# Half the depth of the first output product moved into the graph attention, with two score tiles loaded ahead

## What is computed

```python
edge_index = jnp.stack([src, dst])
xn = _layernorm(x, axis=-1)
x = x + _L0_gnn_ref(xn, edge_index, ...) + _L0_mix_ref(xn[None], ...)[0]
x = x + _L0_ffn_ref(_layernorm(x, axis=-1)[None], ...)[0]

# _L0_mix_ref: linear attention, heads of 64, ends in
out = out.transpose(0, 2, 1, 3).reshape(Bq, Tq, -1)     # 1250 x 1024
return out @ Wo.T + bo

# _L0_gnn_ref: attention over the edges, 4 heads of 64, ends in
out = jax.ops.segment_sum(alpha[..., None] * xl[src], dst, num_segments=n)
out = out.reshape(n, HID)                               # 1250 x 256
return out @ W_up
```

## Time and profile before

| what | value |
|---|---|
| device time, median of 3 runs (2938.48 to 2946.75) | 2941.86 us |
| span of the profiled execution | 2940.1 us |
| TensorE matmul busy over the span | 2668.4 us (91%) |
| `mix0` | 322 to 743 us |
| `out0` | 743 to 902 us |
| `gat_phase` | 902 to 1164 us |

### The profile page before, as it was taken

One profiled execution on the slowest core, in us unless ns is written; L12 is line 12 of the kernel. 1 busy time (PEld: TensorE's weight loads), 2 busy tenths in 40 slices (PEclk: granted clock), 3 DMA queues, 4 the chain that ended last, 5 costly groups with the idle time before them and its releaser, 6 DMA issues. The chain is left out here.

```text
span 2940.1 us, 51469 instructions
## 1 busy us (share of the span) xinstructions
PE 2668.4 (91%) x19570; PEld 2513.2 (85%) x19570; DVE 1606.8 (55%) x3190; ACT 961.0 (33%) x1941; POOL 791.7 (27%) x772
## 2 busy tenths in 40 slices
PE   6677899999885998699979999999999999999788
PEld 6455799999885997588869999899998999999577
DVE  7677677787634886655553222254545332225655
ACT  4466433333203563244431010243434120001243
POOL 0567766777640332122200000000000001100054
PEclk9888999999996998799989999999999999999989
DMA  8933433433739882477753111121112653224382
GB/s 242 289 100 110 115 114 96 116 100 82 209 104 212 225 202 97 117 184 202 193 123 107 40 36 52 30 61 31 58 34 91 185 159 93 65 63 122 121 280 75
DMA packets 202069, 362.93 MB, mean 123 GB/s; under 512 B 33654, under 2 KB 135246, under 8 KB 200595
## 3 DMA queue, kind: packets, MB, share of 16 engines
q1 hardware_dynamic: 165733, 278.89, 32.5%
q0 software_dynamic: 36112, 80.96, 10.9%
HBM read 272.97 MB, written 98.15 MB: 126 GB/s over the span
## 5 line engine op out<-in xcount | busy, mean ns | idle before, releaser
L180 PE MATMUL mix_bank<-sums_w_hi,layer_act_hi 128*125 128x256 f32 x1280 | 359.9, 281 | 0.0
L181 PE MATMUL mix_bank<-sums_w_lo,layer_act_hi 128*125 128x256 f32 x1280 | 359.2, 281 | 0.0
L182 PE MATMUL mix_bank<-sums_w_hi,layer_act_lo 128*125 128x256 f32 x1280 | 358.7, 280 | 0.0
L3184 POOL TENSOR_TENSOR sage_add<-sage_add,sage_bias 125x256 f32<-125x256 f32 x40 | 29.4, 736 | 1193.1 <-DMA sage_add<-resid 1192.9
L181 PEld LDWEIGHTS mix_bank<-sums_w_lo,layer_act_hi 128*125 128x125 f32 x1280 | 237.8, 186 | 0.2
L182 PEld LDWEIGHTS mix_bank<-sums_w_hi,layer_act_lo 128*125 128x125 f32 x1280 | 237.9, 186 | 0.0
L180 PEld LDWEIGHTS mix_bank<-sums_w_hi,layer_act_hi 128*125 128x125 f32 x1280 | 237.7, 186 | 0.1
L567 POOL DMA_INDIRECT scored_ring<-xl,edge_idx x168 | 176.6, 1051 | 157.5 <-issue 138.2
L574 POOL DMA_INDIRECT scores<-edge_e,edge_idx x168 | 174.6, 1039 | 138.5 <-DMA scores<-edge_e,edge_idx 98.9
L567 POOL DMA_INDIRECT scored_ring<-xr,edge_idx x168 | 172.6, 1027 | 51.6 <-issue 51.0
L924 PE MATMUL count_pa<-count_hot_s,count_hot_d 125*125 125x416 bf16 (+1 forms) x624 | 137.5, 383 | 29.9 <-DVE count_hot_s L834 27.8
(11 more groups left out here) (638 smaller groups left out, 8575.0 us busy)
## 6 DMA issues: line engine op xcount, KB each, us to landing
ffn_raw<-in_L_ffn_w_dram SPq DMA_DIRECT2D x16, 2048.0 KB, 13.0
scores<-targets_hole SPq DMA_DIRECT2D x40, 546.9 KB
ffn_raw<-in_L_ffn_W_dram SPq DMA_DIRECT2D x16, 1024.0 KB
gat_sc<-scores SPq DMA_DIRECT2D x6, 2187.5 KB
lasting_raw<-in_L_mix_w_qkv_dram SPq DMA_DIRECT2D x24, 512.0 KB, 3.9
scored_ring<-scores SPq DMA_DIRECT2D x4, 2187.5 KB
layer_slab<-in_L_gnn_W_neigh_dram SPq DMA_DIRECT2D x7, 1024.0 KB
layer_slab<-in_L_gnn_W_self_dram SPq DMA_DIRECT2D x7, 1024.0 KB
```

The lines of the kernel that those rows point to most:

```text
L180: pe.matmul(out, lhs[0], rhs[0], start=first, stop=False)
L181: pe.matmul(out, lhs[0], rhs[1], start=False, stop=False)
L182: return pe.matmul(out, lhs[1], rhs[0], start=False, stop=last)
L3184: pool.tensor_tensor(add[:, u % 2, :], add[:, u % 2, :], bb[:, g * SLAB:(g + 1) * SLAB], ALU.add) \
```

## The change

The depth of the first output product is cut in two. The near half (`NEAR` = 4 parts of 128) stays in `out0`. The far half (`FAR` = 4) is written by `mix0` and `out0` to a new DRAM tensor `far`, laid out by node tile, and multiplied in `gat_phase` inside `product`. `gat_phase` loads the far half of `Wo` (`wide_raw`), turns it by TensorE in eight rounds (`turn_far`, `far_rounded` on ScalarE, `far_rest` on VectorE) during its tile 0, and per tile loads 256 KB of `far` (`mixed`) and splits it (`mix_rounded` on ScalarE, `mix_rest` on GpSimd). The `idle` matmuls are gone. To make room, `DEEP` goes from 3 to 2. The second score tile now has a buffer open since `out0`, and both tiles are loaded there, behind the wait for the last scatter. Batches of edges: 26 in `count_phase`, 13 per two slabs in `mix0`, 6 in `out0`.

```diff
-COUNT_BATCHES = 24
+COUNT_BATCHES = 26
-DEEP = 3
+DEEP = 2
-SLAB_BATCHES = 6
-MIX_END = COUNT_BATCHES + SLAB_BATCHES * (D // (2 * HD))
+SLAB_BATCHES = 13
+MIX_END = COUNT_BATCHES + SLAB_BATCHES * (D // (4 * HD))
...
     def load(self, sp, edges):
         edges.landed(sp)
-        move_rows(sp, self.ring[0:R, 0:N * HEADS], self.rows, self.s_in)
+        move_rows(sp, self.ring[0:R, 0:N * HEADS], self.rows[0], self.s_in)
+        move_rows(sp, self.second[:, :, :].rearrange("p s h -> p (s h)"), self.rows[1], self.s_next)
...
+        w_far = [ph.sb(f"far_{s}", [P, FAR, D], F32R) for s in ("hi", "lo")]
+        mix_raw = ph.sb("mix", [P, 2, FAR, R], F32)
+        mix = [ph.sb(f"mix_{s}", [P, 2, FAR, R], F32R) for s in ("hi", "lo")]
...
+                def mixed(t):
+                    if t >= 2:
+                        sp.wait_ge(s_mlo, t - 1)
+                    sp.dma_start(mix_raw[:, t % 2, :, :], far[t]).then_inc(s_mix[t % 2], 16)
...
+                sp.dma_start(wide_raw[:, :, :], wo.rearrange("(i p) k -> p i k", p=P)[:, :, NEAR * P:D]).then_inc(s_wide, 16)
...
                 for t in range(T):
                     if t + DEEP < T:
                         tile(t + DEEP)
+                        mixed(t + 2)
...
+                def mix_rest(t):
+                    pool.wait_ge(s_mhi, t + 1)
+                    pool.tensor_tensor(mix[1][:, t % 2, :, :], mix_raw[:, t % 2, :, :], mix[0][:, t % 2, :, :].bitcast(F32),
+                                       ALU.subtract).then_inc(s_mlo, 1)
...
+                def far_rest(*rounds):
+                    for i in rounds:
+                        k, c = ROUNDS[i]
+                        cols = slice(c * BANK, (c + 1) * BANK)
+                        dve.wait_ge(s_fhi, i + 1)
+                        dve.tensor_tensor(w_far[1][:, k, cols], pr[:, :], w_far[0][:, k, cols].bitcast(F32), ALU.subtract) \
+                           .then_inc(s_flo, 1)
...
+                def turn_far(i):
+                    k, c = ROUNDS[i]
+                    if i:
+                        pe.wait_ge(s_flo, i)
+                    else:
+                        pe.wait_ge(s_wide, 16)
+                    for j in range(4):
+                        ins = pe.transpose(pr[:, j * P:(j + 1) * P], wide_raw[:, 4 * c + j, k * P:(k + 1) * P], ident[:, :])
+                    ins.then_inc(s_ftr, 1)
...
+                    for k in range(FAR):
+                        mm3(pe, pr[0:R, :], [x[:, t % 2, k, :] for x in mix], [x[:, k, cols] for x in w_far], k == 0, False)
                     for k in range(KH):
-                        ins = mm3(pe, pr[0:R, :], [x[:, k, :] for x in gat], [x[:, k, c * BANK:(c + 1) * BANK] for x in up],
-                                  k == 0, k == KH - 1)
+                        ins = mm3(pe, pr[0:R, :], [x[:, k, :] for x in gat], [x[:, k, cols] for x in up], False, k == KH - 1)
...
-                    if 1 <= t < T:
-                        idle(16)
...
-                    if 1 <= t < T:
-                        idle(10)
...
+                    if first is not None and g == 2:
+                        sp.wait_ge(s_quot, NC)
+                        sp.dma_start(far_part(far, SLABS - 1), output.last.rearrange("p (t r) -> p t r", r=R)).then_inc(s_far, 16)
+                        first.load(sp, edges)
...
-                        if first is not None and g == NSLAB - 1 and half:
-                            first.load(sp, edges)
...
-                        for k in range(KD):
-                            ins = part_product(g, t, k, k == 0, k == KD - 1)
+                        for k in range(KS):
+                            ins = part_product(g, t, k, k == 0, k == KS - 1)
```

More of the change, by code:

```diff
@@ L1057, in keep, with gat_phase @@
         dve.tensor_reduce(self.prob[:, n, :], every, AX.X, ALU.add).then_inc(self.s_prob, 1)
-def gat_phase(nc, first, scores, at, xl, ident, w_up, bias, part, dst, normed, gate_w, prob_out):
+def gat_phase(nc, first, scores, at, xl, ident, w_up, wo, bias, part, far, dst, normed, gate_w, prob_out):
     with Phase(nc, "gat") as ph:
-        sc = [first.tile] + [ph.sb(f"sc{i}", [R, N, HEADS], F32) for i in range(1, DEEP)]
+        sc = [first.tile, first.second]
         cnt = ph.sb("cnt", [R, DEEP, T, R], F32)
@@ L1121, in _ @@
                 tile(1)
+                mixed(0)
                 move_rows(sp, bb, bias.rearrange("(o n) -> o n", o=1).to_broadcast([R, D]), s_bias)
                 rows(0)
-                for t in range(2, DEEP):
-                    tile(t)
+                mixed(1)
                 for t in range(1, ROWS - 1):
@@ L1928, with __init__ @@
 class OutputSlabs:
-    QUARTERS = 4
-    def __init__(self, ph, wo, flip, ahead):
+    def __init__(self, ph, wo, flip, ahead, room=None):
         self.wo, self.flip, self.ahead = wo, flip, ahead
-        self.parts = [ph.sb(f"part{i}", [P, N], F32) for i in range(ahead)]
+        self.depth, self.chunks = (NEAR, 2) if flip else (KD, 4)
+        lent = [] if room is None else [room[:, 0:N], room[:, N:2 * N]]
+        self.parts = [ph.sb(f"part{i}", [P, N], F32) for i in range(ahead - len(lent))] + lent
         self.s_parts = ph.sems("part", ahead)
@@ L1958, in load_parts, with output_phase @@
             sp.dma_start(self.parts[k][:, :], mixt[k * P:(k + 1) * P, :]).then_inc(self.s_parts[k], 16)
-def output_phase(nc, name, act_hi, act_lo, mixt, output, ident, resid, dst, edges=None, turn=None, load=None, room=None, run=None, stage=0, first=None, near=None):
-    WC = OutputSlabs.QUARTERS
+def output_phase(nc, name, act_hi, act_lo, mixt, output, ident, resid, dst, edges=None, turn=None, load=None, run=None, stage=0, first=None, near=None, far=None):
+    WC, KS = output.chunks, output.depth
     DEEP = 4
@@ L1973, in output_phase @@
     with Phase(nc, name, run) as ph:
-        part = output.parts + ([room[:, 0:N], room[:, N:2 * N]] if room is not None else [])
-        part += [ph.sb(f"part{i}", [P, N], F32) for i in range(len(part), DEEP)]
-        w = [output.w0, [ph.sb(f"w1_{s}", [P, KD, SLAB], F32R) for s in ("hi", "lo")]]
+        part = output.parts + [ph.sb(f"part{i}", [P, N], F32) for i in range(output.ahead, DEEP)]
+        w = [output.w0, [x[:, NEAR:KD, :] for x in output.w0] if flip else
+             [ph.sb(f"w1_{s}", [P, KS, SLAB], F32R) for s in ("hi", "lo")]]
+        if first is not None:
+            first.open()
         res = ph.sb("res", [R, 2, T, SLAB], F32)
@@ L1988, in whole_part @@
         def whole_part(k):
[L1989 removed]
+            return part[k % DEEP][:, :] if flip or k < KD - 1 else output.last
         def chunk(c, h):
             if flip:
[L1994 removed]
                 return wide[c % NC][:, :].rearrange("p (k n) -> p k n", n=P), \
[L1996 removed]
+                    [x[:, 0:NEAR, c * P:(c + 1) * P] for x in w[h]]
             return output.quarter(c, w[h])
@@ L2024, in _ @@
                     run.enter(sp, stage)
-                for k in range(output.ahead, KD - 1):
+                for k in range(output.ahead, KS if flip else KD - 1):
                     if k >= DEEP:
@@ L2079, in _ @@
                 todo = edges.turns(dve, MIX_END) if edges is not None else None
-                for _ in range(2):
-                    if todo is not None:
-                        todo.step()
-                for k in range(begun, KD):
-                    if todo is not None and k in (1, 4, 7):
-                        todo.step()
+                for k in range(begun, KS):
                     dve.wait_ge(s_phi, k + 1)
@@ L3896, in gps_kernel @@
                     with Phase(nc, "sums0", run) as sums:
-                        output = OutputSlabs(sums, wo, True, 0)
+                        output = OutputSlabs(sums, wo, True, 2, room=begun.raw)
                         mix_phase(nc, "mix0", *act, wq, wk, wv, [bq, bk, bv], 1e-6, True, ident, mixt[0], output, edges, begun,
-                                  run, 2)
-                        output_phase(nc, "out0", *act, mixt[0], output, ident, x, part, edges, room=begun.raw,
-                                     run=run, stage=3, first=first)
+                                  run, 2, far)
+                        output_phase(nc, "out0", *act, mixt[0], output, ident, x, part, edges,
+                                     run=run, stage=3, first=first, far=far)
                     run.__exit__(None, None, None)
-            gat_phase(nc, first, scores, at, xl, ident, w_up, bo, part, xs[0], y[0], gate0_w, prob)
+            gat_phase(nc, first, scores, at, xl, ident, w_up, wo, bo, part, far, xs[0], y[0], gate0_w, prob)
+            first.beside.ctx.close()
             ffn0.takes(scored)
```

175 lines of the change are left out of this document (126 added, 49 removed).

## The result

The changed kernel takes **3088.3 us** (median of 4 runs, 3077.3 to 3091.9) against 2940.2 us (4 runs) of the kernel before on the same chip: ratio 1.0492, 95% interval 1.0463 to 1.0520. The forecast of slower holds; 3033 us and the range of 2985 to 3070 do not. The profiled execution has a span of 3089.4 us, 149.3 more than that of before.

A forecast was written before the change was run, and what follows sets the result against it. It took GpSimd's gathers and scatters to set when `gat_phase` begins, and a closed score-load loop to pace its tiles after the change. Terms 4 + 13 + 66 + 8 = +91 gave 3033 us, range 2985 to 3070.

The forecast's parts named there:

- term C: Tiles 2 to 9 of `gat_phase`: a closed loop through the score load, 31.0 us a tile against 21.6, +66.
- the landing: Score load in `gat_phase`, from issue to arrival: 11.2 us, or 9 at 277 GB/s.
- The rival at 2989: Tiles 2 to 9: scores land before `halves`, TensorE alone sets 24.7 us a tile, 2989 us; chance 0.13.
- Issue behind `halves`: Tiles 2 to 9: the next score load goes out 18.8 us after `halves`, against 17.6 before.
- The clock: `gat_phase`: TensorE's granted clock falls in its idle gaps; 1 us a tile taken for slower matmuls.
- 33 us a tile: Upper bound for tiles 2 to 9, giving +80; the skill's advice against idle gaps would put it nearer than 30.
- Term A: Up to the start of `gat_phase`: set by GpSimd's gathers and scatters and the loads and stores behind them, +4.
- Term B: Tile 0 of `gat_phase`: eight turning rounds and a later load delay the read of tile 2, +13.
- Term D: Behind tile 9: three products with 5.6 us more each, less 2.9 of `idle` in two; 11, taken as +8.
- Two buffers are enough: Rival for tiles 2 to 9: scores arrive before `halves`, term C is only +22, 2989 us; chance 0.13.
- The product's time comes back: Rival in `out0`: it ends by its matmuls, 55 us sooner; 2930 us with scores hidden too; chance 0.04.

The follow-up runs named there:

- e4: Kernel before with two score buffers in place of three (`DEEP` 3 to 2), nothing else: 3046.4 us, ratio 1.0354.
- e2: Changed kernel loading only the first eighth of each row of scores for tiles 2 to 9: 3012.4 us.
- e1: Changed kernel with the load of scores put ahead of the store of `x` in SyncE's queue: 3017.9 us, ratio 1.0255.
- e13: Changed kernel with the store of `x` issued behind the load of scores, both still waiting for GpSimd's sum: 3072.8 us.
- e14: Changed kernel loading only the first half of each row of scores for tiles 2 to 9: 3045.7 us.
- e6: Changed kernel with 80 idle matmuls ahead of the first product in the iterations of tiles 2 to 9: 3096.6 us.
- e10: Kernel before with two score buffers and the load of scores ahead of the store of `x`: 2972.8 us, ratio 1.0102.
- e16: Kernel before with two score buffers, scores ahead of the store of `x`, and their 13 rows ahead of the 112: 2969.2 us.
- e3: Changed kernel without the 24 far matmuls in each tile's product, their loads and splits kept: 3058.9 us.
- e11: Changed kernel loading only the first tenth of each tile's counts, queued behind the scores, for tiles 2 to 9: 3092.1 us.
- e5: Changed kernel with each score load's 13 rows issued ahead of its 112 rows for tiles 2 to 9: 3082.4 us.

## Why the prediction was right, and where it failed

**The mechanism of term C was right, and the runs show it.** It is a closed loop of `halves`, the products, the copy, the sum, the store, the load and its landing. e4 makes it with the buffer alone, e2 opens it at the landing and e1 at the issue; there are eight waits at `halves`, of 4.3 to 12.7 us (predicted six to eight, of 5 to 9).

**The failed step is the landing: 11.2 us predicted, 16.8 measured.** It stood in the prediction as "between 1010 and 1022 the queue moved 12 x 246 = 2.95 MB [...] so it lands at about 1022". The rate of a window is that of everything on its way; that the first 12 us carry as many bytes as the load has doesn't say that the load's last bytes are among them. The sum didn't close either: 125 x 5000 floats are 2.50 MB in the units of GB/s, not 2.44, and with the store 3.01, more than the 2.95 that had moved. In the changed kernel 0.6 MB queued behind the scores moved ahead of their last bytes. And the window was cut where the rate falls to 73 GB/s. e13 and e14 give the rate that counts, from differences of times: 170 to 189 GB/s. With it the landing would have been 15.9 to 17.7. This is 5.6 x 7 = 39 of the 46 us. The rival at 2989 was weighed by the same rate, and fell further.

**Issue behind `halves`: 18.8 predicted, 20.8 measured.** It holds the fallen clock, that I had as 1 us on its own (e6: 1.4). Together the rest of the loop was 19.8 against 20.8, 7 us in all. "The issue can't move ahead of the last weigh" is true of the counts only: e1 shows that the scores can go out 13 us sooner.

**The clock.** It did fall in the gap (1.00, then 0.50; of the 0.50 that the prediction quotes from before, show nothing, it stands in the window behind them, 916 to 918), and e6 shows the price in the changed kernel, 1.4 us a tile, where I had 1. The rule of the Trainium skill that the prediction names spoke for its 33 us a tile over its 30; the trace agrees with the rule's direction, and the clock was not the miss.

**Term A: +4 and +4.6 agree, partly by luck.** The eleven traced executions with the same code up to there, the changed kernel's own among them, began at 906.9 to 920.3, mean 913; four of the kernel before's side (profiled here, e4, e10, e16) at 900.5 to 905.8, mean 903. The typical term is nearer to +10. The last scatter is issued at 872.07, about where I put it (871 for its landing), and the start comes 34.8 us behind it, where I had 35. `mix0` ended 36 us later (at 779), where I had up to 24.

**Term B: +16.8 for +13.** The load of tile 2 goes out 53.3 us behind the start (960.17; I had 51) and is read 13.4 later (I had 11 to land): half of the miss is the landing again. e4, without the rounds, reads tile 2 6.2 us later than the kernel before does (56.1 against 49.9): that much is the lost buffer's.

**Term D: +15.1 for +8.** I took 8 of a worked-out 11, with 16.9 for the far matmuls and 5.8 off for the `idle` ones. By e3 the far matmuls are 13.1 there. And e3, which has neither kind, still takes 63.8 us against 61.8 before: taking out the `idle` matmuls gave nothing back. The granted clock of that stretch was 0.77 in e3, 0.88 in the changed kernel and 0.91 before, so the two shares can't be told apart cleanly.

**Rivals.** "Two buffers are enough" takes, by e10, the scores ahead of the store, and then still costs 34 us. The rule to double-buffer, from the page of the Trainium skill that the prediction names, did not hold here by itself: with three buffers 21.6 us a tile, with two 35.0 or, reordered, 24.1. "The product's time comes back" didn't come: 480 matmuls left `out0`, and it ended no sooner.

## What to carry to other kernels

Before you take a buffer away, look in the queue at what stands ahead of its refill: here the load's own order in SyncE's queue, behind a store it had no tie to, was worth 70 us (e1), and 74 in the kernel before with two buffers (e10 against e4). Take a transfer's time from its issue to its last byte, or from the difference that some bytes make, never from the mean rate of a window cut to its size; look at the windows behind it as well. And where traces of the same code vary by some 10 us ahead of the place of interest, compare the distances inside the stage.

## What the runs showed of the hardware that I had not expected

DMA engines that are busy to 0.91 moved 150 GB/s in the last 7 us of a load, and 259 in the 10 us before; as differences of bytes and times the load ran at 170 to 189 GB/s. 0.56 MB fewer queued behind the load saved it 0.5 us (e11); 0.51 MB fewer queued ahead saved 3.0 (e13). The order of two parts of one load, 112 rows and 13, was worth 2.1 us (e5), and nothing sure where the scores went out first (e16).

A granted clock that fell in a stall of TensorE did not come back in the same time each time: in e4 it was back some 3 us into the work behind a stall of 11.0 us, and in the next tile only some 16 us behind one of 10.7, and that tile took 38.6 us in place of 34.2.
